# A conditioned adapter on one core: the last down sum ahead of the last additions, and other edits of order

## What is computed

```
dWd = ((h @ Wdd.T + bdd) * 0.1).reshape(B, N, D)     # Wdd: 65536 x 128, 33.6 MB
dWu = ((h @ Wdu.T + bdu) * 0.1).reshape(B, D, N)     # Wdu: 65536 x 128, 33.6 MB
down = relu(einsum('bld,bnd->bln', x, Wd + dWd) + bd)
out = x + einsum('bln,bdn->bld', down, Wu + dWu) + bu
```

## Time and profile before

| | |
|---|---|
| median of 3 runs | 210.28 us (210.24 to 210.34) |
| profiled execution, its own time | 210.96 us |
| its span, first to last instruction | 209.2 us |
| busy: PE, PEld, DVE, ACT, POOL | 168.8, 101.1, 159.4, 58.0, 75.4 us |
| moved by DMA | 85.11 MB, mean 407 GB/s |

### The profile page before, as it was taken

How to read it: one execution, slowest core, us unless ns; L and a number is a source line. 1 busy time by engine, 2 the same in 40 slices (tenths; PEclk the granted TensorE clock), 3 DMA queues, 4 the chain that set the end, 5 groups by cost and what they waited for, 6 DMA issues and landing times.

```text
span 209.2 us, 3093 instructions
## 1 busy us (share of the span) xinstructions
PE 168.8 (81%) x1164; PEld 101.1 (48%) x1164; DVE 159.4 (76%) x88; ACT 58.0 (28%) x105; POOL 75.4 (36%) x60
## 2 busy tenths in 40 slices
PE   1066599757777673999899989999997999998990
PEld 0011173423324140476756847678663665657980
DVE  2868997899999999944844985467969999993471
ACT  2000014101111201043534535544433454534000
POOL 2000000000000000035838816987466779897100
PEclk9999999997969699699999999999999999999997
DMA  6999999999999999999999999999999999999997
GB/s 225 420 417 421 423 425 415 425 423 418 423 423 421 417 404 410 426 423 420 423 423 423 420 414 420 418 426 421 417 418 403 406 420 426 420 387 386 366 362 297
DMA packets 18632, 85.11 MB, mean 407 GB/s; under 512 B 1462, under 2 KB 8635, under 8 KB 9404
## 3 DMA queue, kind: packets, MB, share of 16 engines
q1 hardware_dynamic: 18608, 84.94, 99.8%
q10 hardware_dynamic: 12, 0.00, 0.0%
HBM read 76.55 MB, written 8.39 MB: 406 GB/s over the span
## 4 chain that ended last, share of the span: by engine, by line
DMA 69%; DVE 19%; PE 7%; issue 2%; SPq 0%; DVEq 0%
DMA w<-in_L_cond_Wdu_dram 38%; DMA w<-in_L_cond_Wdd_dram 30%; DVE wt L316 18%; PE bank L668 5%; DVE wt L374 1%; PE dn L644 1%; PE acc L678 1%; PE bank L633 0%; SPq L243 0%; DVE xs L359 0%; PE gt L576 0%; DVE down L348 0%; DVEq L358 0%
## 5 line engine op out<-in xcount | busy, mean ns | idle before, releaser
L316 DVE STREAM_TRANSPOSE wt<-w 128x2048 f32<-128x2048 f32 x63 | 145.5, 2311 | 34.7 <-DMA w<-in_L_cond_Wdu_dram 24.4
L550 PE MATMUL acc<-wt,st 128*32 128x512 f32 x496 | 71.4, 701 | 31.9 <-DVE wt L316 31.9
L499 POOL TENSOR_TENSOR xs<-xs,bu_all 128x1024 f32<-128x1024 f32 x16 | 37.9, 2371 | 102.9 <-PE bank L633 102.9
L550 PEld LDWEIGHTS acc<-wt,st 128*32 128x32 f32 x496 | 14.5, 120 | 70.9 <-DVE wt L316 36.3
L668 PE MATMUL bank<-wu_b,down 128*128 128x128 f32 (+1 forms) x208 | 31.5, 303 | 0.5 <-issue 0.5
L668 PEld LDWEIGHTS bank<-wu_b,down 128*128 128x128 f32 x208 | 27.7, 191 | 7.7 <-issue 5.7
L644 PE MATMUL dn<-xt,wd_b 128*128 128x256 f32 x128 | 30.6, 382 | 0.0
L506 POOL TENSOR_TENSOR xs<-up_s,xs 128x512 f32<-128x512 f32 (+1 forms) x22 | 26.5, 1228 | 7.5 <-ACT up_s L452 7.5
L644 PEld LDWEIGHTS dn<-xt,wd_b 128*128 128x128 f32 x128 | 23.0, 190 | 4.3 <-issue 1.7
L392 ACT ACTIVATE g_rows<-acc 128x512 f32<-128x512 f32 x16 | 9.6, 598 | 48.1 <-PE acc L550 46.4
L434 ACT ACTIVATE xt<-bank 128x512 f32<-128x512 f32 x32 | 17.4, 596 | 8.5 <-PE bank L633 8.5
(11 more groups left out here) (35 smaller groups left out, 36.3 us busy)
## 6 DMA issues: line engine op xcount, KB each, us to landing
w<-in_L_cond_Wdd_dram SPq DMA_DIRECT2D x32, 1024.0 KB, 7.4
w<-in_L_cond_Wdu_dram SPq DMA_DIRECT2D x32, 1024.0 KB, 10.0
xs<-in_x_dram SPq DMA_DIRECT2D x7, 1024.0 KB, 13.3
out_dram<-xs SPq DMA_DIRECT2D x4, 1024.0 KB, 11.2
out_dram<-xs SPq DMA_DIRECT2D x6, 512.0 KB, 4.7
xs<-in_x_dram SPq DMA_DIRECT2D x2, 512.0 KB, 9.7
out_dram<-xs SPq DMA_DIRECT2D x4, 256.0 KB, 4.0
base_d<-in_L_cond_Wd_dram SPq DMA_DIRECT2D x1, 256.0 KB, 7.2
```

The costliest lines, as they stand in the source:

```text
L316: nc.vector.transpose(wt[:, tslot].rearrange("p r (k j) -> p k r j", j=QUAD), w[:, slot, :].rearrange("p (k r h) -> p k r h", r=R, h=QUAD) ...
L499: nc.gpsimd.tensor_tensor(xs[:, b, i0:i0 + UNIT_I], xs[:, b, i0:i0 + UNIT_I], bu_pair, ALU.add).then_inc(bu_added, 1)
L550: last = nc.tensor.matmul(a[TILE * place:TILE * (place + 1)], st[:, r, low * TILE:(low + 1) * TILE], wt[:, slot + h, r], start=low == 0 an ...
```

## The change

It sets `UP_BEFORE_DOWN` from seven units after the loop's last one to one: the last down sum then stands behind unit 20 and in front of units 21 to 33, and ACT's last ReLU in front of its copy of unit 21. The first column half of batch 1 is computed in four units of two row blocks and 256 columns, in place of four of four row blocks and 128 columns; the units are placed anew (`UP_COUNT`), which takes two of them out of chunk 14. Batch 3's last units are put in order of rows, and the last three stores become: second half of row blocks 0 to 3 (512 KB, 1 KB in a row), row blocks 4 and 5 in all columns, row blocks 6 and 7 in all columns (512 KB each, 4 KB in a row); before they were row blocks 4 to 7 in all columns (1 MB, 8 KB in a row) and two second halves of two row blocks (256 KB each, 1 KB in a row). X unit 14 goes from chunk 17 to 15, down sum 13 from 15 to 14, down sum 14 from 18 to 16, and the x piece that unit 14 needs is loaded ahead of chunk 16 instead of 18. TensorE no longer waits for ACT's group copies at the start of a group (the turn of that group has waited for it before), nor for an x piece more than once.

```diff
@@ -54,14 +54,14 @@
 HALF = D // 2
 QD = D // 4
 EARLY = 2
-UNITS = [(b, i, 4, q * QD, QD) for q in range(2) for b in range(EARLY) for i in range(0, I, 4)]
-UNITS += [(b, i, 2, 0, HALF) for b in range(EARLY, B) for i in range(0, I, 2)][:-1]
+UNITS = [(0, i, 4, q * QD, QD) for q in range(2) for i in range(0, I, 4)]
+UNITS += [(b, i, 2, 0, HALF) for b in range(1, B) for i in range(0, I, 2)][:-1]
 UNITS += [(b, i, 4, 2 * QD, QD) for b in range(EARLY) for i in range(0, I, 4)]
 UNITS += [(2, 0, 4, 2 * QD, QD), (2, 4, 2, 2 * QD, QD), (2, 6, 2, 2 * QD, QD)]
 UNITS += [(0, 0, 2, 3 * QD, QD), (0, 2, 2, 3 * QD, QD), (0, 4, 4, 3 * QD, QD)]
 UNITS += [(b, i, 4, 3 * QD, QD) for b in range(1, B - 1) for i in range(0, I, 4)]
-UNITS += [(B - 1, I - 4, 2, HALF, HALF), (B - 1, I - 2, 2, 0, HALF), (B - 1, I - 2, 2, HALF, HALF)]
-UNITS += [(B - 1, i, 2, HALF, HALF) for i in range(0, I - 4, 2)]
+UNITS += [(B - 1, i, 2, HALF, HALF) for i in range(0, I - 2, 2)]
+UNITS += [(B - 1, I - 2, 2, 0, HALF), (B - 1, I - 2, 2, HALF, HALF)]
 UP_UNITS = len(UNITS)
 BANK_COLS = 2 * HALF
 POOL_UNITS = 22
@@ -69,12 +69,12 @@
 
 
 
-TURN_AT = {0: 2, 1: 3, 2: 4, 3: 5, 4: 6, 5: 7, 8: 8, 9: 9, 10: 10, 11: 11, 12: 12, 13: 13, 17: 14}
-DOWN_AT = {0: 1, 1: 2, 2: 3, 3: 4, 4: 5, 5: 6, 6: 7, 9: 8, 10: 9, 11: 10, 12: 11, 13: 12, 15: 13, 18: 14}
+TURN_AT = {0: 2, 1: 3, 2: 4, 3: 5, 4: 6, 5: 7, 8: 8, 9: 9, 10: 10, 11: 11, 12: 12, 13: 13, 15: 14}
+DOWN_AT = {0: 1, 1: 2, 2: 3, 3: 4, 4: 5, 5: 6, 6: 7, 9: 8, 10: 9, 11: 10, 12: 11, 13: 12, 14: 13, 16: 14}
 LAST_DOWN = DOWN_UNITS - 1
 assert list(TURN_AT.values()) == list(range(2, LAST_DOWN))
 assert list(DOWN_AT.values()) == list(range(1, LAST_DOWN))
-UP_COUNT = {8: 1, 9: 1, 14: 2, 16: 1, 19: 2, 20: 2, 21: 1, 22: 2, 23: 1, 24: 2, 25: 1, 26: 1, 27: 2, 28: 1}
+UP_COUNT = {8: 1, 9: 1, 16: 1, 17: 2, 18: 1, 19: 1, 20: 2, 21: 1, 22: 2, 23: 1, 24: 1, 25: 2, 26: 1, 27: 2, 28: 1}
 UP_AT, UP_BEFORE_LAST = {}, 0
 for _t, _n in UP_COUNT.items():
     UP_AT[_t] = list(range(UP_BEFORE_LAST, UP_BEFORE_LAST + _n))
@@ -82,8 +82,8 @@
 
 
 UP_BEFORE_SUM = UP_BEFORE_LAST
-UP_BEFORE_DOWN = UP_BEFORE_SUM + 7
-assert UP_BEFORE_SUM < POOL_UNITS <= UP_BEFORE_DOWN
+UP_BEFORE_DOWN = UP_BEFORE_SUM + 1
+assert UP_BEFORE_SUM < UP_BEFORE_DOWN < POOL_UNITS
 
 
 BANK_USE = [("x", m) for m in range(4)]
@@ -95,15 +95,15 @@
 BANK_USE += [("up", e) for e in range(UP_BEFORE_SUM, UP_UNITS)]
 USE_OF = {use: k for k, use in enumerate(BANK_USE)}
 
-X_LOAD_AT = {0: 0, 2: 1, 4: 2, 6: 3, 10: 4, 12: 5, 14: 6, 18: 7}
+X_LOAD_AT = {0: 0, 2: 1, 4: 2, 6: 3, 10: 4, 12: 5, 14: 6, 16: 7}
 
 
 
 STORES = [(b, slice(0, I), slice(0, HALF)) for b in range(B - 1)] + [(B - 1, slice(0, 4), slice(0, HALF))]
 STORES += [(0, slice(i, i + 2), slice(HALF, D)) for i in range(0, 4, 2)] + [(0, slice(4, I), slice(HALF, D))]
 STORES += [(b, slice(i, i + 4), slice(HALF, D)) for b in range(1, B - 1) for i in range(0, I, 4)]
-STORES += [(B - 1, slice(4, I), slice(0, D))]
-STORES += [(B - 1, slice(i, i + 2), slice(HALF, D)) for i in range(0, 4, 2)]
+STORES += [(B - 1, slice(0, 4), slice(HALF, D))]
+STORES += [(B - 1, slice(i, i + 2), slice(0, D)) for i in range(4, I, 2)]
 
 
 LAST_PARTS = 2
@@ -476,9 +476,11 @@
                     copy_up(e)
             copy_group(2 * GROUPS - 1, 1)
             copy_x_unit(LAST_DOWN)
-            for e in range(UP_BEFORE_SUM, POOL_UNITS):
+            for e in range(UP_BEFORE_SUM, UP_BEFORE_DOWN):
                 copy_up(e)
             copy_down(LAST_DOWN)
+            for e in range(UP_BEFORE_DOWN, POOL_UNITS):
+                copy_up(e)
 
         @block.gpsimd
         def _(pool):
@@ -581,8 +583,6 @@
             def turn(it):
                 for u in range(TURN_CHUNKS):
                     c, s, n = TURN_CHUNKS * it + u, u % SLOTS, u // SLOTS
-                    if s == 0 and later(it, 1):
-                        pe.wait_ge(g_ready, 2 * it + n - 1)
                     if s % PAIR == 0:
                         sum_pair(c, s // PAIR, u % T_RING, acc[n][:])
                     if u == 6 and isinstance(it, int):
@@ -627,7 +627,8 @@
             def turn_x(m):
                 j, c0 = m // 2, m % 2 * BANK_C
                 b, i0 = j // BATCH_UNITS, j % BATCH_UNITS * UNIT_I
-                pe.wait_ge(x_loaded[PIECE_OF[j]], 16)
+                if m % 2 == 0 and (j == 0 or PIECE_OF[j] != PIECE_OF[j - 1]):
+                    pe.wait_ge(x_loaded[PIECE_OF[j]], 16)
                 wait_bank("x", m)
                 for n, (c, i) in enumerate((c, i) for c in range(c0, c0 + BANK_C) for i in range(UNIT_I)):
                     last = nc.tensor.transpose(bank_of("x", m)[:, n * P:(n + 1) * P],
@@ -687,8 +688,6 @@
             down_unit(0)
             for t in range(CHUNKS - PAIR):
                 c, s, g = CHUNKS + t, t % SLOTS, (CHUNKS + t) // SLOTS
-                if s == 0:
-                    pe.wait_ge(g_ready, g - 1)
                 if s % PAIR == 0:
                     sum_pair(c, s // PAIR, t % T_RING_U, acc[g % 2][:])
                 if s == SLOTS - 1:
```

## The result

The change makes the kernel slower by 0.9%: 212.49 us (median of six runs, 211.49 to 212.64) against 210.42 us for six runs of the kernel before, ratio 1.0092 [1.0078, 1.0106]. The prediction, 210.5 with a range up to 211.0, is missed by 2 us.

A forecast was written before the change was run, and what follows sets the result against it. The prediction took the DMA queue of bytes, served without a break, to set the end, not the last addition. Hole +0.3 and end of the list -0.1 gave +0.2 us on 210.28: 210.5, range 209.7 to 211.0.

The forecast's parts named there:

- Store 5 issued near 194.7: Tail, first store needing units 15 and 22: expected out at about 194.7 us instead of 193.5.
- store 14 near 204.1: Tail, last store: expected to be issued at about 204.1 us, with the last addition ending 0.6 us earlier.
- a window around 195 with a DMA share under 0.9: Tail, around 195.3 us: the sign that would show the store queue running dry before store 5.
- the chain sets the end: Rival, tail: stores limited by their arrival, so an earlier last addition carries through; -0.6 us, 209.7; chance 0.17.
- The middle isn't free: Rival, chunks 16 to 19: TensorE carries surplus work to the last pair, delaying the tail; 211.0 us; chance 0.06.
- the hole: Tail, between stores 4 and 5 and before store 7: the queue runs dry; +0.3 us, bounds 0 and 0.7.
- from then on a backlog stands, and the down sum's new place costs no byte.: Tail, from store 7 on: units make bytes faster than the queue serves them, so no further cost.
- The end of the list: Last stores: 512 KB of 1 KB rows move into the stream, 1.46 us instead of 1.57; -0.1 us.
- The halves: Last 1 MB store split into two of 512 KB with 4 KB rows: no loss taken, upper bound 0.35 us.
- the dropped waits: TensorE's repeated waits on g_ready (14) and x_loaded (23): dropping them was taken as worth nothing.
- the queue runs dry: Rival, tail: all engines wait for store 5 and again for store 7; +0.7 - 0.1, 210.9 us; chance 0.24.
- The 3.2 us: Last store: landing time by the skill's fit for a store meeting an empty queue, set against the measured 4.1.

The follow-up runs named there:

- before with early store: Kernel before, with the first column half of batch 3's row blocks 4 and 5 (256 KB) stored behind store 4 instead of inside store 12: 0.9993 (210.39 us).
- change, late down sum: Changed kernel with the last down sum put back between units 26 and 27, all other edits kept: 0.9998 of the kernel before (210.30 us).
- change, early store, waits: Changed kernel with 256 KB of batch 3 stored early, behind store 4, and TensorE's repeated waits put back: 1.0018 of the kernel before (211.21 us).
- change, early store: Changed kernel with 256 KB of batch 3 stored early, behind store 4, down sum still early: 1.0033 of the kernel before (211.29 us).
- before, early down sum: Kernel before with only the last down sum moved, to behind unit 20: 1.0056 (211.32 us).
- before, store 5 held: Kernel before with SP alone holding stores 5 and 6 until DVE has done three units: 1.0092 (212.32 us).
- the late down sum with 130 waits: Changed kernel with the down sum late and 130 already satisfied waits at the start of TensorE's program: 1.0008 of the kernel before (210.58 us).
- the kernel before with 60: Kernel before with 60 already satisfied waits at the start of TensorE's program, nothing else: 1.0017 (210.61 us).
- 32 with the padding: Changed kernel with 64 already satisfied waits in TensorE's program at chunks 0 to 6 of the second matrix: 1.0078 of the kernel before (211.82 us).
- the padded kernel with the load at 198.57 us: Changed kernel with the down sum late and 64 already satisfied waits at chunks 0 to 6 of the second matrix: 1.0024 of the kernel before (210.96 us).
- the padding did not prove it: Kernel before without TensorE's repeated waits, with 32 already satisfied waits at chunks 0 to 6 of the second matrix: 1.0019 (210.80 us).

## Why the prediction was wrong

**Right: the timeline.** Store 5 issued near 194.7 (194.4), store 14 near 204.1 (203.9), DVE's additions near 194.1 and 203.4 (193.90, 203.13), a window around 195 with a DMA share under 0.9 (0.77), 4 KB rows near 400 GB/s (404), the last pair unchanged near 187.15 (186.95). That the queue and not the last addition sets the end is right too: the last addition came 0.85 us earlier, the end later. The rival "the chain sets the end" fell with it. "The middle isn't free" fell as well: TensorE's wait at the last pair grew from 0.25 to 0.79 us, and with the late down sum the whole rest of the change measured 0.9998.

**Mis-sized: the hole.** "I take 0.3, just below the middle, since sixteen engines with a summed share above 1 hardly end in one moment." By store 7, which it counted in, the completions are 0.66 us late, 0.10 of that at store 4 already: 0.56 to 0.66 us, near the upper bound of 0.7. The reason given for the lower value was no reason: a summed share of 1.06 fell to 0.77 all the same.

**Failed: "from then on a backlog stands, and the down sum's new place costs no byte."** The backlog stood; the last store (512 KB, 256 before) took 5.4 us from issue to landing instead of 4.1. But it was served more slowly. The prediction moved its stores at one rate, 358 GB/s, and took that for a property of 1 KB rows. Behind the hole a 512 KB store takes 1.54 us instead of 1.48 (4% more), and the rate is lower in every run with a hole:

```
GB/s at 194 to 196 us                  GB/s at 196 to 204 us    step, us
before with early store        388            372                 1.39
before                         368            362                 1.48
change, late down sum          371            363                 1.45
change, early store, waits     361            352                 1.49
change, early store            326            346                 1.53
before, early down sum         313            343                 1.51
change                         266            338                 1.54
before, store 5 held           209            304                 1.54
```

Of the seven other runs with these stores of 512 KB, five fit in, to within 0.02 us of their neighbours. Two padded ones do not at first sight (347 and 357 GB/s, step 1.52 and 1.51, the late down sum with 130 waits and the kernel before with 60): they have a small gap later, a share of 0.95 and 0.97 at 196 to 198 us, a first step of 1.59 across it and 1.47 to 1.50 behind it. (The last column compares rows of 1 KB alone; the middle one still holds the rest of the hole, most of all for the held store.) The trace shows where the step is lost: a 1 KB packet that starts between 198 and 204 us takes 49.1 ns in the mean after and 47.4 before, 3.7% more, as the step has 4% more; it is 48.2 to 49.1 ns in all seven kernels with the early down sum or the held store, and 46.7 to 47.7 in the eight others with stores of 512 KB (worked out from the traces). What makes the packets longer was not found. That they run in step is not it alone: the sixteen completions of each of stores 8 to 11 lie within 0.2 to 0.3 us in the changed kernel and spread over 0.8 to 1.4 in the kernel before; but with the early down sum in the kernel before they spread over 0.8 to 1.2, and the step is 1.51.

**The end of the list.** -0.1 was taken for it; from store 11 to store 14 the completions show +0.03, 0.88 to 0.91. The halves lost nothing, as taken, and the 512 KB of 1 KB rows that moved forward into the stream gained nothing, since the stream had slowed to 1.52 us for them.

**Not in the sum at all: the dropped waits.** "No idle time in the rows is theirs ... Nothing." As waits they cost nothing, that is right; as instructions they place the last code load. With them dropped, the change has no code load in its tail, and the time around the span is 0.5 us more in the mean of six runs; with about half of the 61 instructions put back (the page counts 31 more with the waits, 32 with the padding), that excess goes, and the ratio falls by 0.0014 or so, with overlapping intervals. That the load which falls behind the end makes the excess is argued, not shown: the change with the late down sum has its load there too, at 209.6, with only 1.77 to 2.23 us around the span. The prediction added a change of the span to a median and so assumed that what lies around the span is constant.

The Trainium skill ("Runtime: NRT & Kernel Launch", section Instruction fetch mechanics) describes the loads: an engine's own DMA queue fetches code in blocks of 16 KiB, 256 instructions, a cost mostly hidden. The trace agrees on the size (16 KB a packet) and, here, not on the last point: the padded kernel with the load at 198.57 us ran 1.0024 where the one without it in the tail ran 0.9998, each on a chip of its own.

**The sum.** Of the 2.0 us by the medians, 1.8 by the means, 0.9 are in the profiled tail by the completions, but that is the quickest of six executions. The spans of all six have a mean of 210.0 us (209.3 to 210.9); the mean of the kernel before, 210.5, less the 1.8 us around its span in every experiment, is 208.7. So 1.3 us lie in the span and 0.5 around it. The order of the tail alone measured 1.2, the early store gave back 1.2. Not placed is a difference of some 0.4 us between the early down sum alone (1.0056) and the change with its waits back (1.0077); the overlapping intervals neither show nor exclude it. Also open: the 0.2 to 0.3% that dropping the waits costs the kernel before; a later code load fits it, the padding did not prove it.

The rival "the queue runs dry" named the right mechanism with the right price for the hole, 210.9. What put the time outside its range too is what it shared with the forecast: one rate for all stores, and a constant around the span. The 3.2 us that the prediction sets beside the last store's 4.1 decide nothing: the Trainium skill ("DMA: Bandwidth & Descriptors", section Anatomy of one DMA) gives that fit for transfers that GpSimd issues, and these stores are issued by SP.

## What to carry to other kernels

When the end is a queue of stores, ask of each reordering first when the first of the final stores goes out, and what is queued ahead of it; finishing the last one earlier is worth nothing while bytes stand in front of it, and a gap costs its own length and then a slower rate behind it. If a reordering must delay the first final store, give the queue something that is ready already: 256 KB issued early gave back 1.2 of 2.0 us here. An edit that only removes waits can still move time (1.0027 here): it moves the code loads, each of which holds one of the sixteen DMA engines for about 1 us. That this is the whole of the cost is argued, not shown; the place to look is the last engine's end, and the time around the span as well as the span.

## What the runs showed of the hardware

- The rate of stores in rows of 1 KB is no constant: 1.39 to 1.54 us for 512 KB, 377 to 340 GB/s, in the eight kernels of the table, at a DMA share of 1.02 to 1.07 between 198 and 204 us. It is lower where the queue had been emptier just before, and the packets of 1 KB are longer there (48.2 to 49.1 ns against 46.7 to 47.7).
- A code load is one 16 KB packet that holds one engine for 0.9 to 1.6 us in the tail. The last engine's end of the last store, behind the mean of the sixteen: 0.6 to 1.0 us in all five kernels with a load at 196.8 to 199.9 us; 0.1 to 0.5 in eight of the nine with the load at 195.2 to 196.5, but 1.0 in the ninth (the kernel before with the early store); 0.1 to 0.4 in the three with no load in the tail. So a late load goes with a late last engine, and is not the only thing that does.
- TensorE's granted clock differed in the early load stage, windows of the changed kernel:

```profile
20.00:40.00 20.00, 14.13 (x92) 6.98 (x96) 17.62 (x10) 4.00 (x7) 0.00 (x0) 0.76 1.02 423
40.00:60.00 20.00, 16.39 (x94) 6.90 (x87) 18.61 (x9) 1.86 (x3) 0.00 (x0) 0.67 1.01 420
```

In the kernel before the same windows were granted 1.00 and 0.90, so here part of the time went at the lower level (1.2 instead of 2.4 GHz). TensorE was busy for 14.1 and 16.4 of 20 us in them. The dropped waits do not decide it: with them put back the two windows have 0.66 and 0.81, with them dropped from the kernel before 1.00 and 0.91. The time was not touched: the DMA share is 1.01 or more in both, and the last weight chunk lands at 185.63 against 185.82.
